# Moving w2's preparation and two fillers in the first slots of an attention pipeline

## The reference

```python
q = bitlinear(x, wq).reshape(B, S, 8, 4, 8)        # 8 key heads, 4 queries each, 8 wide
k = bitlinear(x, wk).reshape(B, S, 8, 8)
v = bitlinear(x, wv).reshape(B, S, 8, 8)
scores = jnp.einsum('bskgd,btkd->bkgst', q, k) * sm_scale
scores = jnp.where(causal, scores, -inf)
probs = softmax(scores)
out = jnp.einsum('bkgst,btkd->bskgd', probs, v)
...
hidden = silu(x @ W1.T) * (x @ W3.T)
hidden = fwht(hidden)                              # Walsh-Hadamard transform, 1024 wide
out = hidden @ W2.T
```

## Time and profile before

| what | us |
|---|---|
| median of three runs (lowest 560.38, highest 565.92) | 564.64 |
| the profiled execution's own time | 565.75 |
| its span in the profile | 563.9 |

### The profile page before, as it was taken

The page is one execution under the profiler, slowest core; times in us unless marked ns, Lnnn a source line. Parts: engine busy times, 40 slices in busy tenths (PEclk is TensorE's granted clock), DMA queues, the critical chain, the costliest instruction groups (busy, mean ns, idle before and its releaser), DMA issues.

```text
span 563.9 us, 9855 instructions
## 1 busy us (share of the span) xinstructions
PE 436.9 (77%) x3348; PEld 303.8 (54%) x3348; DVE 356.6 (63%) x858; ACT 271.6 (48%) x518; POOL 226.7 (40%) x301
## 2 busy tenths in 40 slices
PE   1856799999997759788888152497879799999844
PEld 1634455555553348676777141376658566666433
DVE  5595458878873254946548989688673355555336
ACT  7314757767778424141683154352352355655402
POOL 5870224434566430601310254226627135565600
PEclk9956669999999779989799666678989999999958
DMA  7482071111330029600000000299902245444282
GB/s 215 140 147 96 23 99 45 36 36 45 118 102 7 1 80 331 200 1 1 1 1 1 28 28 28 82 230 244 301 29 99 80 111 148 135 140 117 64 309 77
DMA packets 52032, 56.02 MB, mean 99 GB/s; under 512 B 10244, under 2 KB 42893, under 8 KB 51984
## 3 DMA queue, kind: packets, MB, share of 16 engines
q1 hardware_dynamic: 47536, 46.67, 31.1%
q0 software_dynamic: 4448, 8.73, 4.6%
HBM read 35.61 MB, written 21.73 MB: 102 GB/s over the span
## 4 chain that ended last, share of the span: by engine, by line
PE 51%; DVE 22%; ACT 8%; issue 7%; POOL 4%; DMA 4%; SPq 2%; DVEq 0%; ACTq 0%; POOLq 0%
PE ps L2234 7%; PE ps L1971 5%; PE ps L1950 4%; PE ps L2021 4%; PE ps L1929 4%; PE ps L2257 4%; PE ps L2009 3%; PE ps L2215 3%; PE ps L2010 3%; PE ps L2011 3%; PE ps L1983 2%; DVE st L935 2%; ACT probs L1619 2%; DVE h_lo L1102 1%; PE ps L2349 1%
## 5 line engine op out<-in xcount | busy, mean ns | idle before, releaser
L1619 ACT ACTIVATE probs<-ps 128x512 f32<-128x512 f32 x160 | 87.0, 598 | 42.1 <-PE ps L1950 41.4
L1035 DVE TENSOR_REDUCE negm<-ps 128x2 f32<-128x1024 f32 (+1 forms) x64 | 67.6, 1082 | 16.6 <-PE ps L1939 16.1
L843 POOL DMA_INDIRECT y_slots_scratch<-yblk,ids x48 | 47.0, 979 | 50.0 <-issue 29.5
L677 POOL TENSOR_TENSOR rstd<-ve,halfneg 128x4 f32<-128x4 f32 x15 | 16.2, 1079 | 112.5 <-DVE ve L964 46.9
L1929 PE MATMUL ps<-k_all,q_ring 64*128 64x512 f32 (+3 forms) x256 | 51.9, 412 | 7.0 <-DVE negm L1035 4.2
L1971 PE MATMUL ps<-probs,v_all 128*32 128x128 f32 (+3 forms) x512 | 50.9, 474 | 4.8 <-DVE att L1063 3.2
L1950 PE MATMUL ps<-q_ring,k_all 64*128 64x512 f32 (+3 forms) x256 | 42.8, 392 | 14.8 <-ACT probs L1619 13.2
L1659 ACT CAST h_hi<-hf 128x512 fp32r<-128x512 f32 x28 | 17.4, 620 | 65.7 <-DVE hf L1093 63.5
L1950 PEld LDWEIGHTS ps<-q_ring,k_all 64*128 64x128 f32 x256 | 22.4, 201 | 48.7 <-ACT probs L1619 37.6
L1434 DVE COPY xcol<-ps 128x256 f32<-128x256 f32 x48 | 20.4, 424 | 39.2 <-PE ps L2215 39.2
L1038 DVE TENSOR_REDUCE negm<-ps 128x4 f32<-128x1024 f32 (+1 forms) x32 | 30.6, 959 | 21.2 <-PE ps L1939 21.2
(11 more groups left out here) (327 smaller groups left out, 1339.2 us busy)
## 6 DMA issues: line engine op xcount, KB each, us to landing
x_sorted_scratch<-pad SPq DMA_DIRECT2D x6, 1072.0 KB, 12.3
xblk<-x_sorted_scratch SPq DMA_DIRECT2D x96, 67.0 KB
wgu<-in_moe_w SPq DMA_DIRECT2D x4, 1536.0 KB, 17.5
q_ring<-q_parts_scratch SPq DMA_DIRECT2D x64, 64.0 KB
ycomb<-y_slots_scratch SPq DMA_DIRECT2D x8, 512.0 KB, 6.6
wd<-in_moe_w SPq DMA_DIRECT2D x1, 3072.0 KB, 18.4
sraw<-in_moe_w SPq DMA_DIRECT2D x6, 384.0 KB, 3.1
q_parts_scratch<-qparts SPq DMA_DIRECT2D x4, 512.0 KB, 4.5
```

Source lines behind the costliest of these rows:

```text
L843: pool.indirect_dma_start(out=y_slots, out_offset=bass.IndirectOffsetOnAxis(ap=ids[:, i:i + 1], axis=0), in_=yblk[:, i % YR, :], in_offset ...
L1035: dve.tensor_reduce(negm[:, par, :, hp, qt], pair_of, AX.X, ALU.max, negate=True).then_inc(s1_read, 1)
L1619: act.activation(probs[:, par, u, :], ps[:, col_unit(g, u), :], ACT.Exp)\
```

## The change

ACT rounds the Hadamard matrix instead of DVE, behind `first_high(1)`. ACT calls `ones_rows(1, 0)` and `ones_rows(1, 1)` directly behind the first `w2hi`, no longer in its slots 1 and 2. PE's eight matmuls of the transform stand at the begin of slot 1. DVE's constants become a function that `slots` calls behind slot 2.

```diff
-        def slots(body):
+        def slots(body, third=None):
 
             for n in range(SLOTS):
                 body(n, n % 2, n // 2)
+                if n == 2 and third:
+                    third()
...
-            dve.wait_ge(s_vec, 16)
-            chain.step(dve.tensor_tensor(so2[:, :], wsc[:, 3:4], wsc[:, 3:4], ALU.mult))
...
-            chain.settle()
-            dve.wait_ge(s_w2, 32)
-            dve.tensor_copy(hadr[:, :], had[:, :]).then_inc(w2_split, 1)
-            chain.step(dve.tensor_tensor(ubw[:, :], ubk[:, :], vec[:, WD, :], ALU.subtract))
+            def vector_constants():
+
+                dve.wait_ge(s_vec, 16)
+                chain.step(dve.tensor_tensor(so2[:, :], wsc[:, 3:4], wsc[:, 3:4], ALU.mult))
...
+                chain.settle()
+                chain.step(dve.tensor_tensor(ubw[:, :], ubk[:, :], vec[:, WD, :], ALU.subtract))
...
-            slots(slot)
+            slots(slot, vector_constants)
...
                 if b >= 1:
                     first_high(b)
+                    act.wait_ge(s_w2, 32)
+                    act.copy(hadr[:, :], had[:, :]).then_inc(w2_split, 1)
...
             act.copy(w2hi[:, :, :], w2b[:, :, :]).then_inc(butterfly, 1)
+            ones_rows(1, 0)
+            ones_rows(1, 1)
...
-                if n in (1, 2):
-                    ones_rows(1, n - 1)
...
+                if n == 1:
+
+                    pe.wait_ge(butterfly, 3)
+                    pe.wait_ge(w2_split, 1)
+                    for c in range(4):
+                        for j, half in enumerate((w2hi, w2lo)):
...
-                    if n == 1 and (what, u) == ("rows", 4):
```

More of the change, by code:

```diff
@@ L918, in _ @@
                         .then_inc(q_split, 1)
-            dve.wait_ge(s_vec, 16)
-            chain.step(dve.tensor_tensor(so2[:, :], wsc[:, 3:4], wsc[:, 3:4], ALU.mult))
[L922 to L926, removed]
-            chain.settle()
-            dve.wait_ge(s_w2, 32)
-            dve.tensor_copy(hadr[:, :], had[:, :]).then_inc(w2_split, 1)
-            chain.step(dve.tensor_tensor(ubw[:, :], ubk[:, :], vec[:, WD, :], ALU.subtract))
+            def vector_constants():
+                dve.wait_ge(s_vec, 16)
+                chain.step(dve.tensor_tensor(so2[:, :], wsc[:, 3:4], wsc[:, 3:4], ALU.mult))
+                for q, v in enumerate(MIXES):
+                    chain.step(dve.tensor_scalar(omt[:, q, :], vec[:, v, :], -1.0, 1.0,
+                                                 ALU.mult, ALU.add))
+                chain.step(dve.tensor_tensor(ubk[:, :], vec[:, UK, :], vec[:, BK, :], ALU.add))
+                chain.step(dve.tensor_scalar(nwd[:, :], vec[:, WD, :], -1.0, None, ALU.mult))
+                chain.settle()
+                chain.step(dve.tensor_tensor(ubw[:, :], ubk[:, :], vec[:, WD, :], ALU.subtract))
             def statistics(b, source):
@@ L2035, in slot @@
                     score_rows(0, 1)
+                if n == 1:
[3 more added lines that the diff above has]
+                        for j, half in enumerate((w2hi, w2lo)):
+                            mm = pe.matmul(
+                                ps[:, 4 + c, :], hadr[:, :],
+                                half[:, 2 * c:2 * c + 2, :].rearrange("p c d -> p (c d)"),
+                                start=(j == 0), stop=(j == 1))
+                        mm.then_inc(w2_mm, 1)
                 if has(n, 4) and n % 2:
```

## The result

| | median us | runs | ratio to before, 95% interval |
|---|---|---|---|
| before | 565.28 | 560.38 to 566.45 | |
| after | 558.40 | 557.86 to 559.57 | 0.9886 [0.9847, 0.9925] |
| after, once more beside other kernels | 557.42 (before: 564.84) | 556.80 to 559.25 | 0.9874 [0.984, 0.9908] |

The account below looks back on a forecast made before the run. PE was taken to wait on DVE's first maximum and on exponentials behind ACT's `k_all` fillings. Terms -1.05 - 4.73 - 1.73 - 1.5 + 0.5 = -8.5 took 564.64 to 556.1 us; range 552.5 to 561.5.

Parts of the forecast that it names:

- DVE's constants leave slot 0: Slot 0: without the constants the first maximum starts at 31.85, 2.3 us earlier, and the slot ends at about 39.4.
- The transform waits for `w2lo`: Begin of slot 1: PE waits from 39.4 to 40.65 for POOL's `w2lo`; slot 2 starts at 50.7, worth -1.05 us.
- ACT: Slot 2: fillings fit ACT's hole, the Hadamard rounding costs nothing, and PE's 4.73 us of waiting go: -4.73.
- Second filling, clock and constants in slot 3: Slot 3: PE's wait for an exponential goes, -1.73; TensorE's clock rises earlier, -1.5; seven DVE constants cost +0.5 us.
- SP: SP's stream up to slot 5: its earlier releases let it be through at 77.7, a ceiling of 10.0 us on the gain.
- rival B: Slots 4 and 5: maxima wait behind `load_k`'s transfers or constants cost more; 3 to 5 us lost, 560.1; chance 0.12.
- Sum: Slot 5's start: the terms sum to -8.5 us, so 87.67 becomes 79.2, later than SP's 77.7.
- From there on slots are the same as before: From slot 5's start on: slots keep their old lengths and nothing later has a fixed time, so the -8.5 us stays.
- all behind attention comes earlier by as much: After attention: everything that follows is taken to come earlier by as much as attention does.
- A: Slots 2 and 3: clock stays high from the transform on, up to 3 us less each; 554.6; chance 0.08.
- D: Slot 4 onward: the moved transform no longer lifts the clock, 2.9 us lost a slot, up to 572.2; chance 0.04.
- C: Behind slots 2 and 3: a later wait with a time of its own takes the gain up; 564; chance 0.06.

Follow-up runs that it names:

- e4: The changed kernel with batch 1's four key loads issued one in each of SP's slots 3 to 6 instead of all in slot 3; 554.91 us, ratio 0.9806.
- e9: The kernel before with only the two fillings of `k_all` moved into ACT's hole; 561.10 us, ratio to before 0.9946.
- e6: The changed kernel run and profiled once more, with no edit; 557.42 us, ratio to before 0.9874.
- e8: The changed kernel with batch 1's key loads spread over SP's slots 3 to 6, run once more; 556.63 us, ratio to before 0.9827.
- e12: The changed kernel with the key loads spread and the transform put back behind row unit 4 of slot 1; 554.84 us, ratio to before 0.9846.

## Why the prediction was right, point by point

- *DVE's constants leave slot 0.* Right in mechanism: the first maximum started at 31.08 (forecast 31.85). It was earlier than forecast because the first scores started 0.3 us earlier (30.44 instead of 30.77) and ran at the higher clock (the first pair took 0.50 us instead of 0.79; the granted clock was 1.00 at 30 to 32 us instead of 0.50).
- *The transform waits for `w2lo`.* The step "PE therefore waits from 39.4 to 40.65" failed in its cause. PE waited 2.53 us for group 1's queries, whose DMA I had not put into the sum, and the transform followed at 40.81 without a wait of its own. That the start came out nearly as forecast (40.65) is luck: `w2lo` had ended at 40.3, just before. The rest of slot 1 was shorter than the 6.3 us that I kept, 49.88 - 44.5 = 5.4, so the term was -1.9 instead of -1.05. That goes with the clock, of which I had counted nothing there: at 46 to 48 us, behind the transform, it was 1.00 instead of 0.50.
- *ACT.* Right: the fillings cost nothing in the hole, the 4.73 us went, and slot 2 lasted 8.58 (forecast 8.34). The Hadamard rounding took 0.33 us, and ACT still idled 1.86 us behind it.
- *Second filling, clock and constants in slot 3.* I had -1.73 - 1.5 + 0.5 = -2.7 for this slot; it lasted 9.66 instead of 13.58, which is -3.9. The clock was at 1.00 from 64 us on, so its term, the half of 2.9, was sized too small; and the constants cost 0.7 us on DVE, of which PE shows nothing: column scores and values covered them. None of the seven met a mask of POOL.
- *SP.* Here the forecast was wrong. The step is "79.2, later than SP's 77.7": I took the stretches of SP's stream with their old lengths, as if what is issued behind the key loads took as long as before. The second stretch, 10.0 us before, took 79.62 - 67.37 = 12.25. Issued 0.2 us behind the keys instead of 4.2, group 5's queries landed only at 76.5. That is rival B's mechanism, at the queries where I had it at the maxima, and what I had named as a sign of a wrong step (a wait for `q_ring` of over 1 us). It cost 2.2 us of waiting and 1.6 us in slot 5 at the lower clock; e4 takes both away and e9 brings both in. No run separated the clock from the wait. Nor does one separate SP's issuing (the last of these loads went out at 71.21, in e4 at 69.25) from the transfers themselves.
- *Sum.* Forecast -8.5 at slot 5; measured -8.05 there. That the two are so near is luck: at slot 4's start the gain was 10.3, since slots 1 and 3 gave more than forecast, and the key loads took the excess. "From there on slots are the same as before" failed for slot 5, which ran at the lower clock: 6.5 us were left at slot 6. That all behind attention comes earlier by as much failed too: in the profiles the 6.5 us grew to 9.4 at the table load behind attention (213.25 before, 203.83 after; see the last section) and shrank to 7.6 at the end of the span. So part of the agreement of the time with the forecast is luck too.
- *Rivals.* A fell: the clock was 0.50 at 52 to 54 us. B came true in its mechanism and its price (3 to 5 us forecast, 3.8 measured); the time was better than its 560.1 because slots 1 and 3 had given more. D fell: the clock was 1.00 from 64, with the one dip behind the wait. C fell by the time and by slot 6.

## What to carry to other kernels

When work is moved off an engine's critical stretch, look for the bulk transfer that the longer stretch had covered: here 1 MB of keys for a later phase took back some 3.5 of 10 us, and it did so through small loads queued behind it. Undo the parts also with that conflict removed; only then did their prices add up. For a gain of about 1%, the starts of stages in the profile tell more than the medians of runs, as long as they differ by more than the same kernel's starts do when it is profiled again.

## What was not expected

The end of attention took a different time from kernel to kernel, though none of them changes it, and that hides a few us. ACT's timeline of e4, the last large rounding in attention and the load of the table for the next stage:

```profile
164.57 1.90 ACT L1648 CAST w3hi<-w3raw 128x2048 fp32r<-128x2048 f32 x1
...
203.84 1.28 ACT L1659 ACT_TABLE_LOAD   x1
```

The same two of the changed kernel:

```profile
170.06 1.90 ACT L1646 CAST w3hi<-w3raw 128x2048 fp32r<-128x2048 f32 x1
...
203.83 1.28 ACT L1657 ACT_TABLE_LOAD   x1
```

e4 was 5.5 us ahead and lost all of it (2.2 us of lead are back at the end of the span, 554.1 against 556.3). Windows of e4:

```profile
160.00:180.00 20.00, 14.77 (x126) 7.19 (x122) 4.71 (x9) 13.10 (x23) 13.33 (x20) 0.75 0.02 4
180.00:200.00 20.00, 13.55 (x104) 7.73 (x101) 9.07 (x33) 6.10 (x11) 6.91 (x10) 0.76 0.17 53
```

And of the changed kernel:

```profile
160.00:180.00 20.00, 15.43 (x166) 7.88 (x164) 7.78 (x13) 17.48 (x30) 13.04 (x25) 1.00 0.03 6
180.00:200.00 20.00, 12.33 (x106) 6.30 (x106) 9.85 (x36) 7.00 (x14) 9.74 (x12) 0.91 0.18 53
```

The stretch from that rounding to the table load was 37.0 us in the kernel before, 33.8 after and 35.3 in the same kernel again (e6), 39.3 in e4 and 39.2 in the same kernel again (e8), and 34.7 in e12. The granted clock goes with the length: averaged over the stretch itself it was 0.78, 0.95, 0.81, 0.70, 0.70 and 0.82. No edit touches the instructions there. What makes the clock dip more in one kernel than in another, no run here tells; that e4 and e8 agree speaks against mere chance. So a gain at slot 6 reaches the end changed: in the profiles 6.5 us became 7.6 (after), 11.9 became 9.8 (e4) and 10.5 became 12.1 (e12). Why e8, with the same slot 6 and the same stretch as e4, showed a smaller gain in its median is open; its runs spread from 551.4 to 558.0 us, and the two shortest have the highest granted clocks (0.893 and 0.896, the others 0.879 to 0.888).
